# The attention's inner loops over pairs of tiles, written out

## The chip, the cores and the metric

One Trainium2 chip; the kernel runs on one of its cores, as one launch. The time is that of the device in microseconds (us), from the first to the last instruction of the program. Lower is better.

## What is computed

The reference is a chain of four residual blocks over `x`, which is 8 batches of 1,024 rows of 256 numbers (float32):

```
x = x + attention(layernorm(x))       # 16 heads of 16, with a gated relation bias
x = x + fp8_layer(layernorm(x))
x = x + mamba_block(layernorm(x))     # mixer with a scan, then an MLP
x = x + gated_mlp(layernorm(x))
```

Only the first block is touched. In it, per batch: `q`, `k`, `v` are projections of the normalised rows; the scores of a head are `q·k / sqrt(16)` plus `gate · bias`, where the bias of a row i and a row j is a softmax over three relation logits `li[i] + lj[j]` weighted by three numbers per head; then softmax over j, the product with `v`, and an output projection with a bias.

## The kernel before, in words

`attention()` is the first of four parts that run one after the other (attention, `fp8_layer`, `mixer`, `tail`). It works on tiles of 128 rows: 8 tiles a batch (`NT`), 8 batches (`B`), 64 tiles. For one tile and one head the five engines hand work on in a ring:

- TensorE (`pe_s`, L465) multiplies the queries of the head with the keys of the batch into `ps_s`;
- VectorE (`dve_s`, L317, one instruction a head) adds the bias row to it and takes the minimum;
- ScalarE (`act_e`, L394) takes the exponential;
- TensorE (`pe_t`, L476) transposes the row in 8 pieces into `ps_t`;
- ScalarE (`act_at`, L403) copies the two halves out;
- TensorE (`pe_pv`, L488) multiplies with the values.

`ps_s` has one buffer, so the next head's `pe_s` waits until VectorE has read it. GpSimd and VectorE (`pool_f`, `dve_f`) make the bias rows. Into the same tile the functions `body` weave, at fixed heads `u`, the relation weights of the next tile (`dve_rel` at L289 is issued once a tile, right after head 0; then `act_rel`, `pool_rel` and so on), the projections of the tile that lies one batch ahead, and the output of the tile before. SyncE moves rows, queries and keys by DMA (`sp_x`, `sp_q6`, `sp_xr`, `sp_out`, `sp_parts`, and `sp_keys` once a batch). Engines are synchronised by semaphores; a wait compares a semaphore with a number that grows with the tile, such as `16*t + h + 1`. Where `t` is a number of Python the wait has a constant; where it hangs on a loop's register the sequencer of the engine works the number out first (register instructions at L36 and L43).

The order of all this is fixed by `run` (L561), which every engine calls with its own `body`. `pairs` issues a batch: its tiles 0 and 1, and then a loop (L570) over the pairs 1, 2 and 3, that is tiles 2 to 7, as a hardware loop (`eng.Fori`): the two tiles of a pair stand in the program once, and at the end of an iteration the engine's sequencer branches back to the start. SyncE's loop runs over two pairs only, and its last two tiles stand behind it. The first batch is issued so (with tile 0 and 1 ahead of it), then batches 1 to 6 by an outer loop (L584) of three iterations with two batches each, and the last batch with a loop of its own (L590) over the pairs 1 and 2. So in batches 0 to 6 four of the engines go through the loop of L570 three times a batch, and branch back twice: ahead of tile 4 and ahead of tile 6. In the last batch they branch back once, ahead of tile 4 (tile 60 of 64). The outer loop branches back twice, behind batches 2 and 4.

Of the kernel before, what the change touches and what calls it, by code (L numbers as in the profile page):

```python
# [18 lines left out]
NT = S // P  # L19
# [27 lines left out]
def attention(nc, x_in, wqk, wvg, bqk, rows, ident_in, parts_d, x_out):  # L47
# [13 lines left out]
    with ExitStack() as ctx:  # L61
# [499 lines left out]
        def run(eng, start, project, body, finish, ends=False):  # L561

            def pairs(first, start_i, par, b):
                if start_i == 0:
                    for k in range(2):
                        body(eng, first + k, k, par, k, True, True, True, before=par if k else 1 - par)
                with eng.Fori(1, NT // 2 - ends) as i:  # L570
                    for k in range(2):
                        body(eng, first + 2 * i + k, k, par, 2 * i + k, True, True, True, before=par)
                for k in range(2 * ends):
                    t = first + NT - 2 + k
                    body(eng, t, k, par, NT - 2 + k, True, True, True, before=par, **({"batch": b + 1} if k else {}))

            with eng.Fori(0, NT // 2) as i:
                for k in range(2):
                    project(eng, 2 * i + k, k, 0, 2 * i + k)
            start(eng)  # L580
            for k in range(2):
                body(eng, k, k, 0, k, True, k > 0, True, before=0)
            pairs(0, 1, 0, 0)
            with eng.Fori(0, (B - 2) // 2) as j:  # L584
                for par in (1, 0):
                    b = 2 * j + (1 if par else 2)
                    pairs(b * NT, 0, par, b)
            for k in range(2):
                body(eng, (B - 1) * NT + k, k, 1, k, False, True, True, before=1 if k else 0)
            with eng.Fori(1, NT // 2 - 1) as i:  # L590
                for k in range(2):
                    body(eng, (B - 1) * NT + 2 * i + k, k, 1, 2 * i + k, False, True, True, before=1)
            for k in range(2):
                body(eng, TILES - 2 + k, k, 1, NT - 2 + k, False, True, k == 0, before=1)
            finish(eng)
# [4 lines left out]
        def _(sp):  # L600
# [44 lines left out]
            sp.sem_inc(parts_w, 16)  # L645
            sp_x(sp, 0, 0)
            run(sp, start, project, body, finish, ends=True)

        @block.gpsimd
        def _(pool):  # L650
# [55 lines left out]
            for v in V:  # L706
                nc.gpsimd.memset(v[:, :, :, HD + 1:2 * HD], 0.0)
                nc.gpsimd.memset(v[:, :, :, HD:HD + 1], 1.0).then_inc(v_ok, 1)
            pool.wait_ge(v_ok, 2)
            run(pool, start, project, body, finish)  # L710

        @block.vector
        def _(dve):
# [92 lines left out]
            dve.sem_inc(pm_free, 1)  # L806
            dve.sem_inc(om_free, 1)
            run(dve, start, project, body, finish)

        @block.scalar  # L810
# [1350 lines left out]
```

## Time and profile before

| | |
|---|---|
| median of 3 runs | 6366.53 us (6357.88 to 6370.67) |
| span of the profiled execution, its own time | 6366.2 us |
| busy: TensorE / VectorE / ScalarE / GpSimd | 86% / 73% / 70% / 58% |
| attention | from the start to about 3200 us |
| instruction fetches, queue 8 | 309 packets, 5.06 MB |
| instruction fetches, queue 14 | 205 packets, 1.68 MB |

In the profile PE is TensorE's multiplying, PEld its loading of weights, DVE is VectorE, ACT ScalarE, POOL GpSimd, SP SyncE. A name with a q behind it (PEldq, ACTq) is the sequencer of that engine: it reads the program, works on registers and branches, and hands the engine its instructions. PEclk is the share of full clock that TensorE was granted. The time in brackets behind an instruction is how long its engine had been idle before it, and what ended that; "issue" means that nothing the profile shows was waited for. The profile's DMA part lists, beside the DMA of the program, queues that fetch instructions.

### The profile page before, as it was taken

What the parts mean: (1) busy time and instruction counts of PE and PEld (TensorE: products, weight loads), DVE (VectorE), ACT (ScalarE), POOL (GpSimd) and SP (SyncE); (2) the same over time, 40 slices, a digit from 0 to 9 for tenths busy, and PEclk for the clock granted to TensorE, in tenths of its full rate; (3) what the DMA queues carried; (4) which work ended last, traced back from release to release, by engine and by line L of the source; (5) the groups of instructions that cost most, each with busy time, mean ns of one, the idle gap of its engine ahead of it and who ended that gap; (6) DMA issues with size and microseconds to landing.
All of it is one profiled execution on the core that took longest, in us unless ns stands there. A gap on an engine that the chain in (4) does not pass through costs nothing. (4 is left out here: it accounts for less than half of the span.)

```text
span 6366.2 us, 126141 instructions
## 1 busy us (share of the span) xinstructions
PE 5502.0 (86%) x40354; PEld 3579.2 (56%) x40354; DVE 4670.8 (73%) x6108; ACT 4439.8 (70%) x7115; POOL 3699.2 (58%) x2063
## 2 busy tenths in 40 slices
PE   3688888888888888888879977999999979999999
PEld 3466666666666666665534434555555546666665
DVE  1688988888888888888878958999999961221221
ACT  1698998989899898999936668888888851111111
POOL 2677777777777777777610008999999960000000
PEclk7899999999999999999989989999999999999999
DMA  1212111121211212120035556555555541111110
GB/s 34 43 27 46 29 37 35 27 47 26 47 27 28 45 26 48 28 45 18 13 120 189 213 187 217 204 186 206 189 199 202 206 164 34 33 33 49 33 33 10
DMA packets 470082, 538.37 MB, mean 85 GB/s; under 512 B 251056, under 2 KB 345008, under 8 KB 469568
## 3 DMA queue, kind: packets, MB, share of 16 engines
q1 hardware_dynamic: 469568, 531.63, 27.3%
q8 instruction: 309, 5.06, 0.3%
q14 instruction: 205, 1.68, 0.1%
HBM read 370.18 MB, written 161.35 MB: 83 GB/s over the span
## 5 line engine op out<-in xcount | busy, mean ns | idle before, releaser
L317 DVE CUSTOM_DVE_ANT_0 srow<-srow,ps_s,cur 128x1024 f32<-128x1024 f32 x1024 | 1304.0, 1273 | 262.9 <-PE ps_s L465 180.8
L394 ACT ACTIVATE srow<-srow,nmax 128x1024 f32<-128x1024 f32 x1024 | 1190.9, 1163 | 207.6 <-DVE nmax L317 195.0
L403 ACT COPY AT<-ps_t 128x512 f32<-128x512 f32 x2048 | 1104.9, 597 | 74.8 <-PE ps_t L476 74.0
L476 PEld LDWEIGHTS ps_t<-ident,srow 128*128 128x128 f32 x8192 | 962.7, 143 | 279.1 <-ACT AT L403 84.1
L476 PE MATMUL ps_t<-ident,srow 128*128 128x128 f32 x8192 | 1105.0, 279 | 13.1 <-ACT AT L403 8.7
L1725 POOL TENSOR_TENSOR c_hc<-c_hs,c_cs 128x1024 f32<-128x1024 f32 x432 | 1009.8, 2363 | 60.8 <-DVE c_hs L1827 58.9
L465 PE MATMUL ps_s<-K,Q 96*128 96x512 bf16 x2048 | 632.3, 391 | 440.3 <-DVE nmax L317 318.5
L306 DVE SCALAR_TENSOR_TENSOR srow<-ps_p,rho,R 128x1024 f32<-128x1024 f32 x768 | 975.4, 1270 | 13.7 <-ACT ps_p L357 9.2
L1686 PE MATMUL c_ps_y<-c_hc,c_ident 128*128 128x512 f32 x2048 | 944.8, 594 | 30.0 <-POOL c_hc L1725 17.1
L1827 DVE TENSOR_TENSOR_SCAN c_hs<-c_da,c_pd 128x1024 f32<-128x1024 f32 x384 | 860.2, 2274 | 54.6 <-PE c_pd L1677 54.0
L1770 ACT ACTIVATE c_sT<-c_dxT,c_bT 128x256 f32<-128x256 f32 x1536 | 668.4, 494 | 106.8 <-PE c_pd L1677 96.6
L226 POOL TENSOR_TENSOR srow<-srow,R 128x1024 f32<-128x1024 f32 x256 | 611.8, 2390 | 47.0 <-POOL srow L224 47.0
L488 PE MATMUL ps_o<-AT,V 128*32 128x128 f32 x16384 | 620.0, 281 | 1.1 <-issue 1.1
L1686 PEld LDWEIGHTS c_ps_y<-c_hc,c_ident 128*128 128x128 f32 x2048 | 359.5, 190 | 344.9 <-issue 304.1
L1677 PEld LDWEIGHTS c_pd<-c_ident,c_sT 128*128 128x128 f32 x3072 | 353.8, 141 | 340.2 <-issue 198.4
L1963 POOL TENSOR_TENSOR d_rstd<-d_ve,d_mhalf 128x4 f32<-128x4 f32 x16 | 16.3, 1017 | 899.2 <-DVE d_ve L969 899.2
L465 PEld LDWEIGHTS ps_s<-K,Q 96*128 96x128 bf16 x2048 | 133.2, 98 | 660.3 <-DVE nmax L317 543.6
L1677 PE MATMUL c_pd<-c_ident,c_sT 128*128 128x128 f32 x3072 | 407.3, 276 | 107.0 <-DVE c_hc L1834 79.6
L488 PEld LDWEIGHTS ps_o<-AT,V 128*32 128x32 f32 x16384 | 408.7, 111 | 135.7 <-issue 132.2
L199 POOL TENSOR_TENSOR R<-Dj,RT 128x1024 f32<-128x1024 f32 x128 | 300.7, 2369 | 304.8 <-DVE RT L292 304.8
L1761 ACT ACTIVATE c_da<-c_dt,c_a_neg 128x1024 f32<-128x1024 f32 x384 | 435.8, 1135 | 1.4 <-issue 1.4
L1718 POOL TENSOR_TENSOR c_db<-c_dx,c_bs 128x1024 f32<-128x1024 f32 x128 | 302.0, 2360 | 121.8 <-DMA c_bs<-bc_d 121.8
(196 smaller groups left out, 8361.8 us busy)
## 6 DMA issues: line engine op xcount, KB each, us to landing
c_cs<-bc_d SPq DMA_DIRECT2D x256, 512.0 KB, 4.3
c_bs<-bc_d SPq DMA_DIRECT2D x64, 512.0 KB, 6.7
parts_d<-parts SPq DMA_DIRECT2D x65, 384.0 KB, 3.3
K<-parts_d SPq DMA_DIRECT2D x192, 128.0 KB, 4.6
Q<-parts_d SPq DMA_DIRECT2D x384, 64.0 KB, 2.9
sz_d<-b_sz SPq DMA_DIRECT2D x16, 1024.0 KB, 7.1
xv_d<-b_xv SPq DMA_DIRECT2D x16, 1024.0 KB, 7.7
dt_d<-b_ab SPq DMA_DIRECT2D x16, 1024.0 KB, 4.2
```

What stands on the lines that cost most here:

```text
L306: nc.vector.scalar_tensor_tensor(r[:], ps_p[:], rho[:, h:h + 1], R[k][0][:], ALU.mult, ALU.add).then_inc(fd_ok, 1)
L317: nc.vector.tensor_tensor_reduce(r[:], r[:], ps_s[:], cur[k][:, h:h + 1], BIG, ALU.add, ALU.min, nmax[:, h % NROW:h % NROW + 1]).then_inc( ...
L394: nc.scalar.activation(r[:], r[:], ACT.Exp, scale=-1.0, bias=nmax[:, h % NROW:h % NROW + 1]).then_inc(e_ok, 1)
L403: nc.scalar.copy(AT[h % NAT][:, HG * half:HG * half + HG, :], ps_t[:, half]).then_inc(at_ok, 1)
L465: last = nc.tensor.matmul(ps_s[:, n * 512:(n + 1) * 512], Q6[k][:, h, :], K6[:, h, n * 512:(n + 1) * 512], start=True, stop=True)
L476: last = nc.tensor.transpose(ps_t[:, half, i, :], rows_sb[h % NROW][:, j * P:(j + 1) * P], ident[:])
L488: last = nc.tensor.matmul(ps_o[32 * i:32 * i + 32, j, :], V[par][:, n, h, :], AT[h % NAT][:, n, :], start=(n == 0), stop=(n == NT - 1))
L1677: last = nc.tensor.transpose(pd[:, c, k * P:(k + 1) * P], src[:, k, c * P:(c + 1) * P], ident[:])
L1686: last = nc.tensor.matmul(ps_y[:, c, cut], ident[:], hc[place((n, c)) % NHC][:, cut], start=n == 0, stop=n == NS - 1)
L1725: nc.gpsimd.tensor_tensor(hc[place((n, c)) % NHC][:], hs[place((n, c)) % NHS][:], cs[n % NCS][:], ALU.mult).then_inc(hp_ok, 1)
L1770: last = nc.scalar.activation(sT[i % NSC][:, k, :], dxT[p][:, k, :], ACT.Copy, scale=bT[p][:, k, n:n + 1])
L1827: nc.vector.tensor_tensor_scan(h, gain, push, 0.0, ALU.mult, ALU.add).then_inc(h_ok, 1)
```

## The change

The two inner loops become loops of Python. A batch of eight tiles is then straight-line code on each of the five engines; the outer loop over pairs of batches (L584), and the loop of the first projections ahead of it (L577), stay as they are. The order of the instructions on each engine, the tiles and the semaphores' values are the same. In the first and in the last batch `t` is now a number everywhere, so the waits there have constants; in batches 1 to 6 the numbers hang on the outer loop's register alone.

```diff
-                with eng.Fori(1, NT // 2 - ends) as i:
+                for i in range(1, NT // 2 - ends):
                     for k in range(2):
                         body(eng, first + 2 * i + k, k, par, 2 * i + k, True, True, True, before=par)
...
-            with eng.Fori(1, NT // 2 - 1) as i:
+            for i in range(1, NT // 2 - 1):
                 for k in range(2):
                     body(eng, (B - 1) * NT + 2 * i + k, k, 1, 2 * i + k, False, True, True, before=1)
```

## Rows read from the trace of the kernel before

**Rows 1.** Cores: span and mean granted clock of TensorE.
```profile
core 0: 6366.2 us, clock 0.961
```

**Rows 2.** Windows: length, busy us of PE, PEld, DVE, ACT, POOL, then PEclk, DMA.
```profile
170.00:3200.00 3030.00, 2563.93 (x29426) 1848.76 (x29426) 2598.35 (x3767) 2700.87 (x4103) 2239.87 (x1365) 0.97 0.17 34
...
1143.00:1155.00 12.00, 8.37 (x65) 5.56 (x66) 8.61 (x13) 6.75 (x11) 6.51 (x5) 0.72 0.01 3
1098.00:1110.00 12.00, 8.79 (x104) 6.37 (x108) 11.63 (x18) 10.24 (x16) 7.50 (x6) 1.00 0.04 12
```

**Rows 3.** Waits: us in total, times, longest.
```profile
PE ps_s L465 <- issue: 56.9, 16, 4.9
```

**Rows 4.** Sequencers at the inner loop L570: ns min/median/max, first and last start.
```profile
L570 PEldq COMPARE_BRANCH  x21: 83/3966/5353, 392.0 to 2839.5; - x21
...
L570 ACTq COMPARE_BRANCH  x21: 40/45/50, 392.0 to 2839.6; - x21
```

**Rows 5.** TensorE's sequencer at the last batch's loop L590 and the outer loop L584.
```profile
L590 PEldq COMPARE_BRANCH  x2: 78/2118/4157, 3011.5 to 3098.3; - x2
...
L584 PEldq COMPARE_BRANCH  x3: 76/3765/4809, 1329.4 to 2839.7; - x3
```

**Rows 6.** Timeline, start of tile 3 of batch 2: start, us, instruction, idle before.
```profile
1098.97 0.61 PE L465 MATMUL ps_s<-K,Q 96*128 96x512 bf16 x2 [1.32 <-DVE nmax L317]
...
1100.83 1.27 DVE L317 CUSTOM_DVE_ANT_0 srow<-srow,ps_s,cur 128x1024 f32<-128x1024 f32 x1
```

**Rows 7.** Timeline, start of tile 4 of batch 2, behind a branch back.
```profile
1146.10 0.60 PE L465 MATMUL ps_s<-K,Q 96*128 96x512 bf16 x2 [3.39 <-issue]
...
1146.88 1.28 DVE L317 CUSTOM_DVE_ANT_0 srow<-srow,ps_s,cur 128x1024 f32<-128x1024 f32 x1 [0.91 <-issue]
```

**Rows 8.** L289, once a tile: first and last start, tile 1 to 4, batches 0 and 2.
```profile
L289 DVE TENSOR_SCALAR RT<-Dj,cur x4: 815/870/1042, 258.9 to 394.0; 128x1024 f32<-128x1024 f32 x3, 128x1024 f32 x1
...
L289 DVE TENSOR_SCALAR RT<-Dj,cur x4: 874/880/885, 1008.4 to 1143.9; 128x1024 f32 x4
```

**Rows 9.** L289, the same, tile 4 to 7, batches 0 to 6.
```profile
L289 DVE TENSOR_SCALAR RT<-Dj,cur x4: 854/879/901, 394.0 to 533.1; 128x1024 f32<-128x1024 f32 x2, 128x1024 f32 x2
L289 DVE TENSOR_SCALAR RT<-Dj,cur x4: 844/875/898, 768.4 to 907.0; 128x1024 f32 x4
L289 DVE TENSOR_SCALAR RT<-Dj,cur x4: 854/883/891, 1143.9 to 1286.1; 128x1024 f32 x4
L289 DVE TENSOR_SCALAR RT<-Dj,cur x4: 868/880/897, 1523.6 to 1664.9; 128x1024 f32 x4
L289 DVE TENSOR_SCALAR RT<-Dj,cur x4: 871/895/901, 1901.6 to 2044.0; 128x1024 f32 x4
L289 DVE TENSOR_SCALAR RT<-Dj,cur x4: 854/878/885, 2283.4 to 2422.4; 128x1024 f32 x4
L289 DVE TENSOR_SCALAR RT<-Dj,cur x4: 871/875/892, 2657.2 to 2796.4; 128x1024 f32 x4
```

**Rows 10.** L289, last batch: tile 1 to 4, and tile 4 to 5.
```profile
L289 DVE TENSOR_SCALAR RT<-Dj,cur x4: 747/748/749, 2884.9 to 3013.6; 128x1024 f32<-128x1024 f32 x4
...
L289 DVE TENSOR_SCALAR RT<-Dj,cur x2: 747/748/749, 3013.6 to 3057.6; 128x1024 f32<-128x1024 f32 x2
```

**Rows 11.** DMA queues: packets, MB, share; first row 391 to 577 us, others 577 to 767.
```profile
q8 instruction: 20, 0.33, 0.8%
...
q8 instruction: 15, 0.25, 0.6%
q14 instruction: 12, 0.10, 0.2%
```

**Rows 12.** Timeline, VectorE, head 11 of tile 2 in batches 2 and 3.
```profile
1082.57 1.28 DVE L317 CUSTOM_DVE_ANT_0 srow<-srow,ps_s,cur 128x1024 f32<-128x1024 f32 x1 [1.79 <-PE ps_s L465]
...
1462.31 1.28 DVE L317 CUSTOM_DVE_ANT_0 srow<-srow,ps_s,cur 128x1024 f32<-128x1024 f32 x1 [1.43 <-PE ps_s L465]
```

**Rows 13.** TensorE's sequencer at the loop of `tail`, L1905.
```profile
L1905 PEldq COMPARE_BRANCH  x7: 76/208/208, 5380.1 to 6216.2; - x7
```

## The prediction

> **What bounds the kernel now.** I read the page first: 6366.2 us of span [rows 1], a median of 6366.53 over three runs. The two agree within 0.4 us, so the sum below is made against the span and needs no correction. The change touches only the attention, up to about 3200 us. There no engine is full: ScalarE is busy for 2700.87 of 3030 us (89%), VectorE for 2598 (86%), TensorE for 2564 (85%) [rows 2]. The rest is waiting, and the question is how much of that waiting comes from the loops.
>
> So I went to the waits next. The reader is to see one odd row: TensorE's score multiplication at L465 was idle 16 times with nothing to wait for ("issue"), 56.9 us in all, up to 4.9 us at a time [rows 3]. Everything else at L465 waits for VectorE. A handful of long stops without a releaser points at TensorE's own sequencer. The view of line L570 names it: the 21 branches at the loop's end take 83 ns at the least, 3,966 ns in the median and up to 5,353 ns on TensorE, against 45 ns on ScalarE [rows 4] (the rows of VectorE, GpSimd and SyncE are like ScalarE's). Of three branches a batch two go back and one falls through; the short ones are the seven that fall through. The last batch has one of each, 4,157 and 78 ns [rows 5]. So 14 + 1 = 15 branches back stop TensorE's supply of instructions for about 4 us each, some 60 us.
>
> Not all of this reaches the end. The timeline shows how much does, at the start of a tile. Where no branch lies ahead, head 1's scores start when VectorE has read head 0's, after 1.32 us of idleness, and VectorE goes on without a gap [rows 6]. Behind a branch back the same multiplication comes after 3.39 us of idleness, and VectorE stands for 0.91 us [rows 7]; then the transposes come late, and ScalarE with them. In the 12 us behind that branch VectorE is busy for 8.61 us and ScalarE for 6.75, where the undisturbed tile has 11.63 and 10.24; the granted clock of TensorE was 0.72 there and 1.00 in the other [rows 2]. So the lowered clock after the stop is a part of the price, and it is counted in what follows, since that is measured on whole tiles.
>
> **The change part by part.**
>
> *The 15 branches back of TensorE go.* L289 is issued once a tile, and its starts are a clock for tiles. From tile 1 to tile 4 of a batch there are three tiles and no branch back: 135.1 us in batch 0 and 135.5 in batch 2 [rows 8], which are the shortest and the longest of the seven batches 0 to 6. I take 135.3. From tile 4 to tile 7 there are three tiles of the same work with two branches back: 139.1, 138.6, 142.2, 141.3, 142.4, 139.0 and 139.2 us [rows 9], in sum 981.8. The difference is 981.8 − 7 × 135.3 = 34.7 us. In the last batch three tiles without a branch take 128.7 us, 42.9 each, and the tile behind its branch back takes 44.0 [rows 10]: 1.1 us. Together 35.8 us, or 2.4 us for each of the 15. The other 1.6 us of each stop are TensorE's slack at that place, the 1.32 us of [rows 6] first of all.
>
> What is late next: nothing new. A tile behind a vanished branch begins like that of [rows 6], where TensorE waits for VectorE's result.
>
> *The branches back of the other engines go.* They take 45 ns on ScalarE and lie beside work in hand: the instruction of VectorE at such an end, L306, lasts 1.27 us. I cost them at nothing; what they do cost is inside the 35.8 already, since the same tiles are measured.
>
> *The waits get constants in batches 0 and 7.* The register instructions are handled by the sequencers while the engines work. Tiles 2 and 3 of batch 0 hang on one register, those of batch 2 on two, and three tiles take 135.1 and 135.5 us [rows 8]; the 0.4 between them is another thing, found below. So I put the registers at nothing; if that 0.4 were theirs after all, it would be 0.2 us for each of 24 tiles that lose one, another 5 us of gain.
>
> *SyncE.* It loses 8 branches back (one a batch). It issues the queries one tile ahead, so no one waits for it within a batch. Nothing; were that cover gone, 8 stops like TensorE's would be 32 us of SyncE, also a gain.
>
> *What stays.* The outer loop branches back twice, for 3.8 and 4.8 us on TensorE [rows 5], where the first tile of a batch waits for its keys anyway. The keys at the start of a batch are loaded as before.
>
> *Straight-line code has to be fetched.* This is the one part that could cost. In two pairs of tiles inside the loop 20 blocks of code came on queue 8 and none on queue 14; in two pairs of straight code 15 and 12 [rows 11]. Queue 8 brings more in the loop, so it is TensorE's, which has to fetch its iteration again; queue 14 then serves the other engines, which keep theirs. After the change each pair that now runs from the kept code fetches 6 blocks more: 15 pairs, 90 blocks. How much one block can stop an engine the trace shows at one place: head 11 of tile 2, where VectorE stands for 1.79 us in batch 2 and for 1.43 in batch 3, the same work in the two copies of the batch in the program [rows 12]. So one bubble of 0.36 us. It happened in three of the seven undisturbed stretches (135.5 against 135.1 or 135.2), that is once in seven tiles, and my base of 135.3 a stretch contains it. From below the cost is then nothing, from above 0.36 us for one block of VectorE in each of 30 tiles, 11 us. I take the base as it is, because tiles 1 to 3 are just such code as tiles 4 to 7 will be.
>
> Sum: 6366.2 − 35.8 = 6330.4; I say 6331.
>
> **The rivals.**
>
> *The fetches give it back (slower).* Place: the 90 blocks that VectorE, ScalarE, GpSimd and SyncE must now fetch within a batch. If each stopped the ring by the 0.36 us of [rows 12], that is 32 us, and the time 6363: no change. The point at which the sign turns is 35.8 / 90 = 0.40 us a block. If one in four were as bad as a branch back of TensorE, 2.4 us on the path, that is 23 × 2.4 = 55 us: 6331 + 55 = 6386. For it: these engines have no fetches at all in the loop now. Against it: tiles 1 to 3 of all batches run on freshly fetched code, in 135.1 to 135.5 us for three, so the fetch runs ahead.
>
> *The branch is not the cause (no change).* Something else at tiles 4 and 6, a DMA or the clock, holds TensorE, and the sequencer is only seen waiting. Then only the bare branches go, 15 × 0.083 us = 1.2 us: 6365. The Trainium skill's page "Advanced Engine Details and Errata", section "Control Flow Timing", gives a compare-and-branch about 108 ns; as an estimate by that page, 15 of them are 1.6 us and the time 6365 as well. Against it: tile 2, which begins a pair without a branch back, shows none of the delay, and the long branches are just those that go back.
>
> *The code behind moves (slower or less gain).* The loops of the later parts branch back 15 times too (4, 5 and 6 times), at 208 ns on TensorE in `tail` [rows 13]. The program becomes longer ahead of them. If their code then lay so that TensorE has to fetch at each branch, as in L570, each would cost 3,966 − 208 ns, 56 us in all: 6331 + 56 = 6387; with the six of `tail` alone, 6331 + 23 = 6354. The Trainium skill's page "Runtime: NRT & Kernel Launch", section "Instruction fetch mechanics", says that a taken branch stalls for a fetch when its target is outside the two pages held; that would allow such a shift. Against it: none of these branches is long now (the rows of the other two loops are like that of `tail`), whatever place their code has.
>
> **How the numbers follow.** The forecast has a chance of 0.85. Its own range is 6319 to 6346: upward the 11 us of bubbles and 4 us, by which the highest run lies over the median; downward 9 us, by which the lowest run lies under it, and half of the 5 us of registers. The fetches 0.07, of which 0.03 near no change and 0.04 slower; the branch not the cause 0.05; the code behind 0.03, slower. The range for 8 in 10 is 6318 to 6350; above, it reaches on to a gain of which the fetches have eaten nearly half. A measurement of this kernel tells about 0.2%, 12.7 us, from no change. Faster by more: 0.85. Within: 0.03 + 0.05 = 0.08. Slower: 0.04 + 0.03 = 0.07.
>
> **What would show it.** Right: L465 has one "issue" stop instead of 16; no branch at L570 or L590; tiles 4 to 7 take 135 to 136 us as tiles 1 to 4 do; the granted clock stays 1.00 at the start of tile 4; queue 8 has about 37 blocks fewer (2.5 for each of 15 pairs), queue 14 about 90 more. Wrong: gaps of VectorE or ScalarE ended by "issue" in tiles 2 to 7, longer starts of batches, or long branches at L1051, L1595 or L1905 on TensorE.

## The result and the profile after

The changed kernel takes 6330.07 us (median of 4 runs, 6328.16 to 6331.17) against 6366.52 before. The ratio is 0.9944, with a 95% interval of 0.9932 to 0.9956: about 36 us less, where 35.8 were forecast. The profiled execution has a span of 6327.4 us, 38.8 less than the one before.

The branches of the inner loops are gone; those of the outer loop and of the later parts are what they were. TensorE's sequencer at L584 and L1905 in the kernel after (ns min/median/max, first and last start), beside [rows 5] and [rows 13]:

```profile
L584 PEldq COMPARE_BRANCH  x3: 83/4657/4692, 1315.4 to 2807.3; - x3
...
L1905 PEldq COMPARE_BRANCH  x7: 76/208/223, 5342.0 to 6178.1; - x7
```

In the view of waits the row of [rows 3] (L465 idle 16 times without a releaser) has no successor. The start of tile 4 of batch 2, which was [rows 7], now has the form of [rows 6]: the timeline of the kernel after.

```profile
1136.05 1.17 DVE L289 TENSOR_SCALAR RT<-Dj,cur 128x1024 f32 x1
...
1136.19 0.61 PE L465 MATMUL ps_s<-K,Q 96*128 96x512 bf16 x2 [1.32 <-DVE nmax L317]
...
1138.34 1.26 DVE L317 CUSTOM_DVE_ANT_0 srow<-srow,ps_s,cur 128x1024 f32<-128x1024 f32 x1
```

TensorE waits for VectorE for 1.32 us, not for its own program. In the 12 us from there the windows show ScalarE busy for 10.72 us (6.75 behind the branch, 10.24 in the undisturbed tile) and the granted clock at 1.00, which is the higher of its two levels (2.4 GHz), where its mean was 0.72 [rows 2]:

```profile
1136.00:1148.00 12.00, 9.15 (x108) 6.45 (x108) 11.64 (x18) 10.72 (x16) 7.49 (x6) 1.00 0.04 13
```

The clock of tiles: L289 from tile 4 to tile 7 of batches 0 to 6, which answer [rows 9], and in the last batch from tile 4 to 5, which answers the second of [rows 10].

```profile
L289 DVE TENSOR_SCALAR RT<-Dj,cur x4: 855/870/873, 396.8 to 531.3; 128x1024 f32<-128x1024 f32 x4
L289 DVE TENSOR_SCALAR RT<-Dj,cur x4: 876/1040/1181, 764.5 to 900.2; 128x1024 f32 x4
L289 DVE TENSOR_SCALAR RT<-Dj,cur x4: 873/1032/1183, 1136.0 to 1272.1; 128x1024 f32 x4
L289 DVE TENSOR_SCALAR RT<-Dj,cur x4: 873/1032/1174, 1511.3 to 1647.1; 128x1024 f32 x4
L289 DVE TENSOR_SCALAR RT<-Dj,cur x4: 871/1020/1171, 1882.0 to 2019.0; 128x1024 f32 x4
L289 DVE TENSOR_SCALAR RT<-Dj,cur x4: 873/1026/1175, 2256.6 to 2392.3; 128x1024 f32 x4
L289 DVE TENSOR_SCALAR RT<-Dj,cur x4: 867/1016/1171, 2627.9 to 2763.9; 128x1024 f32 x4
...
L289 DVE TENSOR_SCALAR RT<-Dj,cur x2: 748/750/752, 2980.9 to 3023.7; 128x1024 f32<-128x1024 f32 x2
```

The seven stretches sum to 134.5 + 135.7 + 136.1 + 135.8 + 137.0 + 135.7 + 136.0 = 950.8 us, where they were 981.8: 31.0 us less. The tile of the last batch is 42.8 after 44.0. Batch 4 is about 1 us over the others (137.0), by one tile; why is not known. The same rows show something new: in batches 1 to 6 L289 itself takes up to 1.18 us, while the median in batch 0 is still 0.87.

The instruction fetches moved as expected in direction, less in size (page of the kernel after; 309 and 205 packets before):

```profile
q8 instruction: 279, 4.57, 0.3%
q14 instruction: 272, 2.23, 0.1%
```

### The profile page after: what moved, and what is told of

Same layout as the page of the kernel before. It is cut to its first block and busy times, and to the rows that moved or that the text cites. A ratio compares the mean times of both kernels' runs of the same rounds, so it can differ in the third digit from the quotient of the medians.

```text
span 6327.4 us, 123950 instructions
## 1 busy us (share of the span) xinstructions
PE 5472.2 (86%) x40354; PEld 3561.7 (56%) x40354; DVE 4677.3 (74%) x6108; ACT 4442.3 (70%) x7115; POOL 3699.4 (58%) x2063
## 5 line engine op out<-in xcount | busy, mean ns | idle before, releaser
L317 DVE CUSTOM_DVE_ANT_0 srow<-srow,ps_s,cur 128x1024 f32<-128x1024 f32 x1024 | 1304.8, 1274 | 231.8 <-PE ps_s L465 140.4
L476 PE MATMUL ps_t<-ident,srow 128*128 128x128 f32 x8192 | 1090.3, 276 | 14.1 <-ACT AT L403 10.6
L1725 POOL TENSOR_TENSOR c_hc<-c_hs,c_cs 128x1024 f32<-128x1024 f32 x432 | 1010.3, 2365 | 61.7 <-DVE c_hs L1827 61.7
L465 PE MATMUL ps_s<-K,Q 96*128 96x512 bf16 x2048 | 624.7, 387 | 430.8 <-DVE nmax L317 367.3
L226 POOL TENSOR_TENSOR srow<-srow,R 128x1024 f32<-128x1024 f32 x256 | 611.3, 2388 | 55.2 <-POOL srow L224 55.2
L465 PEld LDWEIGHTS ps_s<-K,Q 96*128 96x128 bf16 x2048 | 131.5, 97 | 652.7 <-DVE nmax L317 581.1
```

Source lines behind the costliest of these rows:

```text
L317: nc.vector.tensor_tensor_reduce(r[:], r[:], ps_s[:], cur[k][:, h:h + 1], BIG, ALU.add, ALU.min, nmax[:, h % NROW:h % NROW + 1]).then_inc( ...
L465: last = nc.tensor.matmul(ps_s[:, n * 512:(n + 1) * 512], Q6[k][:, h, :], K6[:, h, n * 512:(n + 1) * 512], start=True, stop=True)
L476: last = nc.tensor.transpose(ps_t[:, half, i, :], rows_sb[h % NROW][:, j * P:(j + 1) * P], ident[:])
L1725: nc.gpsimd.tensor_tensor(hc[place((n, c)) % NHC][:], hs[place((n, c)) % NHS][:], cs[n % NCS][:], ALU.mult).then_inc(hp_ok, 1)
```

## The experiments

Times are medians in us, with the lowest and the highest run in brackets; a ratio is that to the kernel before, with its 95% interval. In the diffs, `looped` chooses between the hardware loop and the loop of Python.

**Which engine's loop it was.** Two kernels split the change: e1_pe_only and e2_others_only.

```diff
+            def inner(hi, step):
+                if looped:
+                    with eng.Fori(1, hi) as i:
+                        step(i)
+                else:
+                    for i in range(1, hi):
+                        step(i)
...
-            run(dve, start, project, body, finish)
+            run(dve, start, project, body, finish, looped=True)   # and ScalarE, GpSimd, SyncE
```

> The loops written out on TensorE alone; the four other engines keep both hardware loops. Theory (the loss was TensorE's fetch behind a branch to a far target): the whole gain, 6325 to 6331 us, L465 with at most one idle stop of over 3 us without a releaser. Rival (part of the gain came from the other engines' branches and from waits with constants): a third of the 36 us missing or more, 6342 us or above.

It took 6324.39 (6320.67 to 6325.28; ratio 0.9933, interval 0.9917 to 0.9950): the whole gain. The median lies 0.6 us below the range that the theory gave. It is lower than that of the change itself too, but the intervals of the two overlap; the tiles say it better: the seven stretches from tile 4 to 7 sum to 946.3 us, 4.5 less than in the kernel after. No multiplication at L465 stops without a releaser any more. Batch 2's row, where L289 is short again (of this kernel's trace):

```profile
L289 DVE TENSOR_SCALAR RT<-Dj,cur x4: 872/878/912, 1135.2 to 1270.5; 128x1024 f32 x4
```

The other half has `looped=True` on TensorE alone.

> The other half: TensorE keeps its loops, the four other engines have them written out. Theory: no gain, 6364 to 6372 us, TensorE's branches back at the inner loops still about 4 us each, tiles 4 and 6 some 2.4 us longer than tiles 3 and 5. Rival: 6354 us or below.

It took 6363.42 (6361.6 to 6370.4; ratio 0.9998, interval 0.9988 to 1.0008): no gain. The median lies 0.6 us below the range that the theory gave. The stops are all there; TensorE's sequencer at the two inner loops (here one line, L565), and the waits:

```profile
L565 PEldq COMPARE_BRANCH  x23: 78/3970/5426, 392.9 to 3096.9; - x23
```

```profile
PE ps_s L465 <- issue: 56.9, 16, 5.0
```

The seven stretches sum to 977.9 us. So the gain is TensorE's, and written-out code on the other four engines gains nothing in sum. In its parts it does two small things: three tiles of batch 0 fall from 135.1 to 134.7 us, where the waits got constants, and L289 takes 1.15 to 1.20 us in tiles 2, 4 and 6 of batches 1 to 6, as in the kernel after.

**The branch, or the way to its target.** e3_short_branch is the kernel after, with a branch back put in again at the same 15 places, but to a target a few instructions away.

```diff
                 for i in range(1, NT // 2 - ends):
                     for k in range(2):
                         body(eng, first + 2 * i + k, k, par, 2 * i + k, True, True, True, before=par)
+                    if short is not None and i < NT // 2 - 1:      # TensorE only
+                        with eng.Fori(0, 2):
+                            eng.sem_inc(short, 1)
```

> The kernel after, with a loop of two rounds around one semaphore increment put into TensorE's program at the 15 places where it branched back before; it branches back once at each place, to a target a few instructions away. Theory (the distance costs, for the fetch): branches of about 0.2 us, 6330 to 6334 us, tiles 4 and 6 as long as in the kernel after, within 0.3 us. Rival (any branch back stops TensorE's supply): some 4 us at each branch and 6360 us or above.

It took 6329.76 (6323.81 to 6333.03; ratio 0.9940, interval 0.9924 to 0.9957), like the kernel after (the range that the theory gave began at 6330). TensorE's sequencer at the added loops (L575 in batches 0 to 6, L598 in the last; half of the branches go back, half fall through):

```profile
L575 PEldq COMPARE_BRANCH  x28: 76/144/242, 391.3 to 2715.8; - x28
```

```profile
L598 PEldq COMPARE_BRANCH  x2: 67/151/235, 2978.0 to 2978.5; - x2
```

A branch back of TensorE takes 0.21 to 0.24 us when its target is near, and the tiles do not feel it: the seven stretches sum to 949.6 us, as in the kernel after. The 4 us belong to the far target. That they are a fetch is shown by the packets of queue 8. In the trace of the kernel before, a packet of 16,384 bytes starts within each of the 15 branches back, 0.5 to 1.6 us behind the branch's start, and has arrived 1.3 to 1.7 us before its end; none starts within a branch that falls through or goes back near, and none within the 30 short branches here. The branch ahead of tile 4 of batch 2, in the DMA view of the kernel before from 1142 to 1146 us:

```profile
q8 instruction: 1, 0.02, 2.3%
```

**What L289 waits for.** In the kernel after L289 takes 1.15 to 1.20 us in tiles 2, 4 and 6 of batches 1 to 6 (1.09 to 1.24 in tile 0) and 0.83 to 0.90 in the odd ones. GpSimd's timeline shows where the two differ, at the start of tile 4 and of tile 5 of batch 1:

```profile
762.71 2.37 POOL L226 TENSOR_TENSOR srow<-srow,R 128x1024 f32<-128x1024 f32 x1 [0.48 <-POOL srow L224]
...
807.79 2.37 POOL L226 TENSOR_TENSOR srow<-srow,R 128x1024 f32<-128x1024 f32 x1 [0.18 <-POOL srow L224]
```

VectorE's timeline, the L289 that begins under each of them:

```profile
764.45 1.18 DVE L289 TENSOR_SCALAR RT<-Dj,cur 128x1024 f32 x1
...
809.81 0.90 DVE L289 TENSOR_SCALAR RT<-Dj,cur 128x1024 f32 x1
```

In the first pair L226 ends 0.63 us after L289 has begun, in the second 0.35; both times L289 ends 0.55 us after L226. The Trainium skill, page "SBUF — State Buffer", section "SBUF: two separate sides", says that VectorE and GpSimd share a pair of ports, and that of two instructions that both need it the one that starts first holds it to its end while the other blocks. The trace agrees: in all 56 tiles in which L289 meets an L226, from tile 1 of batch 0 to tile 0 of the last batch, it ends 0.55 or 0.56 us after L226, however long the two overlap, and it takes 0.75 us in the six tiles in which it meets none. What is late is GpSimd, by 0.3 us every second tile: its sequencer stands for 0.40 us ahead of the first of these L226 and for 0.10 ahead of the second. Counted in the trace, its program has exactly 64 instructions a tile in the written-out batches 1 to 6 (two more behind an outer branch); the stops are 128 instructions apart (130 across such a branch), and a packet of queue 14 of 8,192 bytes starts 0.6 to 1.8 us behind each of the 24 stops. If a packet holds 128 instructions, two tiles are one packet, and its end falls on the same place of every even tile. The test, e4_pool_shift, moves that place.

```diff
             pool.wait_ge(v_ok, 2)
+            for _ in range(24):
+                pool.sem_inc(pool_own, 1)
             run(pool, start, project, body, finish)
```

> The kernel after, with 24 semaphore increments put into GpSimd's program ahead of the tiles. In the kernel after L289 takes 1.17 us in the even tiles of batches 1 to 6 and 0.87 in the odd ones, because GpSimd's L226 starts 0.28 us later there. Theory (GpSimd has 64 instructions a tile, so a fetched block of 128 ends at the same place of each even tile, and its change costs 0.28 us): the end of the block moves away from L226, L289 takes 0.87 us in the even tiles too, tiles 2, 4 and 6 take 45.05 in place of 45.34 us, 18 x 0.3 = 5 us less in all, about 6325 us. Rival (the registers' work or VectorE's own supply): L289 stays at 1.17 us, 6330 us.

It took 6323.49 (6319.72 to 6329.58; ratio 0.9933, interval 0.9917 to 0.9950). L289 over batch 1, first in this kernel, then in the kernel after:

```profile
L289 DVE TENSOR_SCALAR RT<-Dj,cur x8: 864/876/896, 629.5 to 944.8; 128x1024 f32 x8
```

```profile
L289 DVE TENSOR_SCALAR RT<-Dj,cur x8: 873/1028/1181, 629.0 to 945.3; 128x1024 f32 x8
```

No L289 is over 0.90 us there, nor in batches 2 to 6; the one of tile 5 of batch 0 is 1.16 instead. The eight starts span 315.3 us in place of 316.3. So 24 instructions that do nothing take the stop out of the way. The total's interval overlaps that of the kernel after, so the gain rests on the tiles, not on the median: from tile 1 to tile 7 of batches 1 to 6 this kernel needs 1,622.4 us by L289's starts, 6.4 less than in the kernel after.

**What is left in the attention.** In e5_full the outer loop is written out as well.

```diff
-            with eng.Fori(0, (B - 2) // 2) as j:
+            for j in range((B - 2) // 2):
```

> The outer loop over pairs of batches written out too, on all engines: no branch back and no register number is left in the attention's 64 tiles. Theory (two prices are left in the kernel after: the registers' numbers, since its batches 0 and 7, with constants alone, run 44.85 and 42.75 us a tile against 45.05 and 42.90 with registers, and the outer branch, behind which tile 7 of batches 2 and 4 takes 47.4 us): tiles 1 to 6 of batches 1 to 6 at 44.85 us, tile 7 of batches 2 and 4 at about 45, some 14 + 7 = 21 us less than the kernel after, about 6309 us. Rival (the keys at each batch's start swallow what a batch gains, and constants are worth nothing): 6325 us or above.

It took 6303.48 (6300.04 to 6305.57; ratio 0.9901, interval 0.9884 to 0.9917): the fastest kernel here, 27 us under the kernel after and some 6 under what I had expected. Its tile rate, tile 1 to 3 of batch 2, two tiles in 89.7 us, and the start behind the first outer branch, tile 7 of batch 2 to tile 1 of batch 3, against the same in the kernel after:

```profile
L289 DVE TENSOR_SCALAR RT<-Dj,cur x3: 871/873/877, 995.4 to 1085.1; 128x1024 f32<-128x1024 f32 x3
...
L289 DVE TENSOR_SCALAR RT<-Dj,cur x3: 857/865/877, 1264.5 to 1363.5; 128x1024 f32<-128x1024 f32 x3
```

```profile
L289 DVE TENSOR_SCALAR RT<-Dj,cur x3: 884/897/1192, 1272.1 to 1375.8; 128x1024 f32 x3
```

A tile with constants takes 44.85 us, one with the outer register 45.05 or 45.34. From tile 1 to tile 7 of batches 1 to 6 the kernel after needs 1,629 us by L289's starts and this one 1,616, 13 us less. Not all of that is the registers' price: GpSimd's program has 47 instructions a tile here, its stops no longer meet L289, and 6.4 of the 13 had gone in e4_pool_shift already. Some 7 us, 0.2 a tile, are left for constants. The two starts behind an outer branch are 99.0 for 103.7 and 99.3 for 102.2, 7.6 us less. Both prices are real, and both were put at nothing in my prediction.

**The same on the next loop.** e6_full_mixer writes out the mixer's loop over its batches as well, on all engines.

```diff
-            with eng.Fori(1, B - 1) as b:
+            for b in range(1, B - 1):
                 for p in range(PAIRS):
                     body(PAIRS * b + p, b, p, False, False)
```

> As e5_full, and the mixer's loop over batches (L1595) written out as well. In the kernel after ScalarE goes on 4.4 to 6.2 us after its branch back there and GpSimd 3.3 to 3.8 us, 5 times each, where GpSimd is busy for 94% of the stage. Theory (the far target costs any engine a fetch, and on GpSimd, which is the bound there, most of it reaches the end): 10 to 17 us less than e5_full. Rival (buffers ahead of GpSimd cover it): within 4 us of e5_full.

It took 6308.91 (6307.05 to 6313.88): no gain over the 6303.48 of e5_full, rather a loss of 5, which neither the theory nor the rival had said. Two more kernels tell the engines apart, each writing out the same loop on some engines only.

```diff
-        def pairs(eng, body):
+        def pairs(eng, body, out=False):          # out: a loop of Python
...
-            pairs(pool, body)
+            pairs(pool, body, out=True)           # e7: GpSimd and ScalarE; e8: TensorE
```

> As e5_full, with the mixer's loop over batches written out on ScalarE and GpSimd alone, the two engines whose branch back there is long. Theory (e6_full_mixer lost 5 us to e5_full because TensorE, whose branch back there is short, now has to fetch its code while the DMA queues are half busy): as fast as e5_full or up to 4 us faster, 6299 to 6304 us. Rival (any engine's written-out code costs there, or the 5 us are spread between runs): 6306 to 6310 us.

> As e5_full, with the mixer's loop written out on TensorE alone. Theory (TensorE's code from memory is what costs there): the 5 us of e6_full_mixer, 6307 to 6311 us. Rival: within 2 us of e5_full, 6302 to 6306 us.

They took 6306.84 (6305.34 to 6308.23) and 6310.16 (6310.03 to 6310.86). The first lies outside the range that I gave it and inside the rival's, so its total speaks against the theory, though its lowest run and the highest of e5_full touch. Where its 3 us lie is not found. The stage says more: the multiplications of GpSimd (L1725, or L1732 where lines moved) from the first to the last start, in e5_full, e6, e7 and e8.

```profile
L1725 POOL TENSOR_TENSOR c_hc<-c_hs,c_cs x432: 2339/2368/2437, 3781.1 to 5133.3; 128x1024 f32<-128x1024 f32 x144
```

```profile
L1725 POOL TENSOR_TENSOR c_hc<-c_hs,c_cs x432: 2338/2366/2426, 3782.6 to 5139.1; 128x1024 f32<-128x1024 f32 x144
```

```profile
L1732 POOL TENSOR_TENSOR c_hc<-c_hs,c_cs x432: 2339/2367/2425, 3780.2 to 5133.1; 128x1024 f32<-128x1024 f32 x144
```

```profile
L1732 POOL TENSOR_TENSOR c_hc<-c_hs,c_cs x432: 2342/2367/2458, 3782.6 to 5139.1; 128x1024 f32<-128x1024 f32 x144
```

That is 1352.2, 1356.5, 1352.9 and 1356.5 us. In the eight traces in which TensorE keeps this loop, the kernels before and after among them, the stage takes 1352.2 to 1354.2 us. So with TensorE written out it is 2 to 4 us longer, twice the same, and with ScalarE and GpSimd alone it is unchanged: their long branches there do not reach the end. TensorE's loading of weights, idle without a releaser, goes from the first row (e5_full) to the second (e8):

```profile
PEld c_pd L1677 <- issue: 197.5, 508, 21.6
```

```profile
PEld c_pd L1684 <- issue: 346.9, 653, 23.2
```

Queue 8 brings 42 packets in this stage (3780 to 5140 us) in place of 16. So code that TensorE has kept is handed on faster there than code that it must fetch. That the busy DMA of this stage is the reason was my guess in the expectation, and no run shows it.

## Why the prediction was right, step by step

**The 15 branches back: right, in place and size.** They were 35.8 us by tiles. e1_pe_only, which takes these away and adds fetches on TensorE alone, has 946.3 us in the seven stretches and 42.9 in the last batch's tile; against 981.8 and 44.0 that is 36.6 us, 2.4 a branch.

**The other engines' branches at nothing: right** (e2_others_only), but the row that I read it from cannot show it. On ScalarE the branch's row stays at 45 ns also where the next instruction of the loop comes late. The mixer's loop in the kernel after, one branch back (4300 to 4306 us):

```profile
L1595 ACTq COMPARE_BRANCH  x1: 45/45/45, 4300.9 to 4300.9; - x1
L1595 ACTq FUSED_REGOPS  x1: 50/50/50, 4305.3 to 4305.3; - x1
```

That is 4.4 us to the next instruction. Behind L570 in the kernel before it is 0.2 to 0.3 us on all four engines, so the price was small there; behind the outer loop's L584 it is 2.8 to 5.8 us.

**Straight-line code at the base of tiles 1 to 3: right in size, wrong in place.** I priced the fetches of the other engines between 0 and 11 us and took tiles 1 to 3 as the model for tiles 4 to 7. The change pays 3.7 us of it: the stretches are 950.8 us where 7 × 135.3 = 947.1 had been forecast. But most of it is not the bubble that I read from [rows 12], 0.36 us of VectorE at head 11. It was GpSimd's block end, handed on to VectorE through the ports, in every even tile of batches 1 to 6 (tile 2 included, so the base moved too). The bubble of [rows 12] is there as well, at another place. In the kernel before, L317 starts 0.48 us after VectorE's sequencer has met its semaphore in batches 2, 4 and 6, and 0.13 in batch 3, and a packet of queue 14 starts 0.64 us behind each time, as behind GpSimd's stops. By these marks it is VectorE's own block end, which is what I took it for. In the kernel after the same stop is at L250 in tile 6 of batches 2, 4 and 6, where VectorE's idle time before it is 0.15 us in the other tiles:

```profile
1234.42 0.18 DVE L250 BATCH_NORM_AGGREGATE mv<-stats 128x2 f32<-128x6 f32 x1 [0.50 <-DVE stats L248]
```

In batches 2 and 6 that tile takes 45.65 us, where the others with a long L289 take 45.35.

**Registers at nothing: wrong, though small here.** In batches 0 and 7, where the change brings constants, a stretch of three tiles fell from 135.1 to 134.8 us and from 128.7 to 128.2. The step that failed compared tiles with one register and with two [rows 8], never registers with constants. e5_full shows the size: 0.2 us a tile. It is not TensorE's: with TensorE's loops alone written out (e1_pe_only) a tile of the last batch stays at 42.9 us; with those of the others (e2_others_only) it takes 42.7 where no branch lies ahead.

**The starts of batches: not forecast.** From tile 7 to the next batch's tile 1, the seven starts sum to 697.1 us before and 692.6 after. The other kernels with the outer loop have 691.5 (e1_pe_only), 693.9 (e4_pool_shift), 696.4 (e2_others_only, which keeps TensorE's inner loops) and 696.0 (e3_short_branch, which has no far branch there). So these starts differ by as much between traces of kernels without the far branches, and the 4.5 us are not shown to come from the change. They are luck, about as large as the 3.7 that the bubbles took. Outside the tiles the trace of the kernel after reaches the L289 of tile 0 later by 3.4 us and ends sooner by 4.8 us behind the last L289, and nothing shows that the change does either. So the total came out within 1 us of the forecast, which is better than its parts.

**The rivals.** The fetches did not give the gain back; 67 more packets came on queue 14 (272 for 205, not 90), and 30 fewer on queue 8 (37 had been worked out). The branch was the cause. The later loops did not move out of reach: medians of 208 to 212 ns at L1051, L1595 and L1905, 207 to 208 before.

## What to carry to other kernels

On TensorE a hardware loop's price stands in the profile as the time of the branch at its end. On the other engines that row is 34 to 74 ns in any case; there look at when the next instruction of the loop starts, and on every engine at what goes idle without a releaser behind the branch. Then measure whole tiles with and without a branch ahead of them, because slack takes a part (here 1.6 of 4 us). Write out only what pays: TensorE's loop with its far target did, the other engines' short ones did not, and in the mixer, where TensorE's branch was short, its written-out code was slower. Constants in place of registers are worth a little in every tile and the outer branches had their price, so writing out the attention's last loop as well made the fastest kernel.

## What the hardware showed that I had not expected

GpSimd's supply of instructions can set VectorE's time: a stop of 0.3 us in GpSimd's sequencer, every 128 instructions, made an instruction of VectorE 0.3 us longer (1.18 for 0.90 us) in the even tiles of six batches, until 24 instructions without work moved it. And straight-line code was not always the faster form: the mixer's stage took 1356.5 us with TensorE's code written out and 1352.2 to 1354.2 from the loop.
